# Row statistics joined on GpSimd for eight tiles at once, and value weights of two sequences from one product, spread by DMA transfers, in a decoder layer on one core

## What is computed

```python
proj = einsum('btd,ed->bte', x, W_in); gate, val = proj[..., :D], proj[..., D:]
v = depthwise_conv5(val) + conv_b
y = scan(h = tanh(a) * h + sigmoid(gate) * v)              # over the 1024 tokens
res = x + y @ W_out.T
x1 = layernorm(x + layernorm(res) * ln_w + ln_b)           # first and second norm

k, v = rmsnorm(ctx) @ Wk.T, rmsnorm(ctx) @ Wv.T            # 64 context rows a sequence
for _ in range(3):                                         # slots = x1 at first
    q = rmsnorm(slots) @ Wq.T
    attn = softmax(q @ k.T / 16, over the 1024 slots); attn /= attn.sum(over the context)
    slots = gru(attn @ v, slots)                           # gates need (attn @ v) @ gru_wih.T
x2 = layernorm(x1 + slots)
out = layernorm(x2 + x2 + x2 @ expert_w[argmax(x2 @ gate_w.T)])
```

## Time and profile before

| | |
|---|---|
| three runs | 555.04, 557.29, 557.83 us (median 557.29) |
| the profiled execution | 557.2 us, its span 555.4 us |
| mean granted TensorE clock | 0.972 |
| busy: PE, DVE, ACT, POOL | 507.8, 438.9, 343.8, 250.5 us |
| busy in the first 240 us: PE, DVE, ACT, POOL | 211.0, 200.5, 155.6, 70.6 us |

### The profile page before, as it was taken

How to read it: one execution, slowest core, us unless ns; L and a number is a source line. 1 busy time by engine, 2 the same in 40 slices (tenths; PEclk the granted TensorE clock), 3 DMA queues, 4 the chain that set the end, 5 groups by cost and what they waited for, 6 DMA issues and landing times.

```text
span 555.4 us, 7269 instructions
## 1 busy us (share of the span) xinstructions
PE 507.8 (91%) x2174; PEld 366.0 (66%) x2174; DVE 438.9 (79%) x794; ACT 343.8 (62%) x608; POOL 250.5 (45%) x217
## 2 busy tenths in 40 slices
PE   6999986978779999899999999999997999979992
PEld 2465552845557687488768867885885788767771
DVE  2899999997799477989967985897677567868783
ACT  3657539786598474667466656765663766557453
POOL 0133050400223256556935664574335156737776
PEclk9999999899898999999999999999997999989997
DMA  8960202210021032000000000002111136255752
GB/s 299 316 194 2 76 1 76 76 44 33 0 77 63 15 77 77 0 2 0 2 1 1 0 0 1 2 1 76 40 38 39 38 128 235 91 159 157 222 153 71
DMA packets 28101, 39.98 MB, mean 72 GB/s; under 512 B 7421, under 2 KB 19838, under 8 KB 27776
## 3 DMA queue, kind: packets, MB, share of 16 engines
q1 hardware_dynamic: 24656, 31.10, 18.0%
q0 software_dynamic: 3408, 8.43, 4.1%
HBM read 25.70 MB, written 16.83 MB: 77 GB/s over the span
## 4 chain that ended last, share of the span: by engine, by line
PE 51%; DVE 6%; issue 6%; POOL 4%; ACT 3%; DMA 1%; SPq 0%; POOLq 0%; ACTq 0%; DVEq 0%
PE psum L1452 35%; PE psum L1542 7%; PE psum L1255 3%; PE psum L1394 2%; PE psum L1513 2%; PE psum L1340 1%; POOL gru L1005 1%; DVE gru L1865 1%; POOL sorted_rows L1035 1%; DVE slots_full L1867 1%; POOL out L1043 1%; POOL slots_lo L1020 1%; PE psum L1352 1%; DVE gru L1845 1%; PE psum L1416 1%
## 5 line engine op out<-in xcount | busy, mean ns | idle before, releaser
L1452 PE MATMUL psum<-slots_hi,w_hh 128*128 128x512 f32 x560 | 181.5, 406 | 1.2 <-ACT gru L752 1.2
L1452 PEld LDWEIGHTS psum<-slots_hi,w_hh 128*128 128x128 f32 x560 | 104.5, 191 | 27.8 <-issue 4.2
L1005 POOL TENSOR_TENSOR gru<-slots_full,gru 128x512 f32<-128x512 f32 x43 | 65.7, 1529 | 111.8 <-ACT gru L758 111.8
L1452 PE MATMUL psum<-slots_lo,w_hh 128*128 128x512 f32 x280 | 112.0, 400 | 0.0
L1452 PE MATMUL psum<-at,v_ih_pair 128*128 128x512 f32 x288 | 91.4, 402 | 5.0 <-DVE at L1744 3.1
L758 ACT ACTIVATE gru<-gru,vec 128x512 f32<-128x512 f32 x48 | 34.7, 722 | 58.7 <-DVE gru L1845 58.6
L1452 PEld LDWEIGHTS psum<-at,v_ih_pair 128*128 128x128 f32 x288 | 53.7, 190 | 21.9 <-DVE at L1744 3.4
L1838 DVE SCALAR_TENSOR_TENSOR gru<-psum,vec,gru 128x512 f32<-128x512 f32 x48 | 35.9, 747 | 36.0 <-PE psum L1452 30.2
L1138 PE MATMUL psum<-early_hi,w_in 128*128 128x512 f32 x128 | 57.9, 611 | 5.3 <-DMA early_hi<-in_xT 5.2
L1452 PEld LDWEIGHTS psum<-slots_lo,w_hh 128*128 128x128 f32 x280 | 53.4, 191 | 12.9
L1865 DVE TENSOR_TENSOR gru<-gru 128x512 f32<-128x512 f32 x47 | 43.7, 929 | 7.2 <-POOL gru L1005 3.7
(11 more groups left out here) (249 smaller groups left out, 878.3 us busy)
## 6 DMA issues: line engine op xcount, KB each, us to landing
gathered<-sorted_rows SPq DMA_DIRECT2D x39, 129.0 KB, 2.5
x_scratch<-slots_full SPq DMA_DIRECT2D x8, 512.0 KB, 3.0
x_block<-x_scratch SPq DMA_DIRECT2D x8, 512.0 KB, 4.1
early_hi<-in_xT SPq DMA_DIRECT2D x3, 1024.0 KB, 5.4
x_tm<-in_x SPq DMA_DIRECT2D x4, 512.0 KB, 6.3
slots_full<-expert_plus SPq DMA_DIRECT2D x1, 2048.0 KB, 10.3
sorted_rows<-gru SPq DMA_DIRECT2D x1, 1032.0 KB, 11.7
early_hi<-in_xT SPq DMA_DIRECT2D x2, 512.0 KB, 4.6
```

Of the source, the lines that this page charges most:

```text
L1005: pool.tensor_tensor(DF(u), full[:, c, seq(k, h), blk(j)], X(u), ALU.subtract).then_inc(d_pool, 1)
L1452: last = pe.matmul(psum[:, bank, :], w, d, start=start and i == 0, stop=stop and i == len(pairs) - 1, skip_group_check=begun or late)
```

## The change

Statistics: bn_stats now writes to `st6` with room for both norms, and the joins leave VectorE. GpSimd makes them for eight tiles at once in six instructions (`gather_halves`): the sum of the two halves' means and spreads, the difference of the means, scaled, squared and added, and minus half the sum of the means. It also makes the offsets and mean squares (`first_offsets`, `second_offsets`). `window` and `row_roots` scale by 1/256 in their Ln. `add_bias` is split so that the first join stands ahead of its fourth addition.

Value weights: `v_sb` holds each sequence once, so one product's 128 rows are 64 of one sequence and 64 of the next; i = 0 to 3 is all there is. ScalarE copies rounded part and rest into three buffers `value_part`, used in turn (parts n = 0 to 7), and SyncE spreads each part with four transfers into `v_ih_pair`: each sequence's 64 rows to both halves of the partitions. A copy of part n > 2 waits until the four transfers of part n - 3 have landed (`vp_out`).

```diff
+        value_parts = [sb2(f"value_part{i}", [P, G3 // 2], F32R) for i in range(3)]
+        def high_part(i):
+            return 4 * (i // 2) + i % 2
+                def spread_value(pair):
+                    for n in range(4 * pair, 4 * pair + 4):
+                        w, h = n // 2 % 2, n % 2
+                        sp.wait_ge((vp_hi, vp_lo)[w], 2 * pair + h + 1)
+                        for b in range(2):
+                            for to in range(2):
+                                sp.dma_start(v_ih[pair][half(to), b, w, h * HG:(h + 1) * HG].bitcast(F32),
+                                             value_parts[n % 3][half(b), :].bitcast(F32)).then_inc(vp_out[n % 3], 16)
...
                 load_fm(3)
                 load_tm(2)
+                spread_value(0)
                 load_tm(3)
+                spread_value(1)
...
-                        act.wait_ge(agg1, NT * n1)
+                        act.wait_ge(agg1, 6 * n1)
...
+                def free_part(n):
+                    if n > 2:
+                        act.wait_ge(vp_out[n % 3], 64 * (n // 3))
...
                 def value_low(i):
-                    b, h = i // 2, i % 2
                     act.wait_ge(vp_sub, i + 1)
-                    act.activation(vp(1, b)[:, h * HG:(h + 1) * HG], psum[:, value_bank(i), 0:HG],
+                    free_part(high_part(i) + 2)
+                    act.activation(value_parts[(high_part(i) + 2) % 3][:], psum[:, value_bank(i), 0:HG],
...
-                value_high(4)
-                value_high(5)
                 first_rows(2)
-                value_low(4)
-                value_low(5)
                 new_slots(1)
                 spread_roots(0, OB)
                 low_slots(1)
-                value_high(6)
-                value_high(7)
                 window(4)
-                value_low(6)
-                value_low(7)
...
+                def gather_halves(n, done, b):
+                    even, odd = st6[:, n, :, 1:3], st6[:, n, :, 4:6]
+                    pool.tensor_tensor(joint[:, n], even, odd, ALU.add).then_inc(done, 1)
+                    pool.tensor_tensor(apart[:, n], even[:, :, 0], odd[:, :, 0], ALU.subtract).then_inc(done, 1)
+                    pool.wait_ge(done, 6 * b + 2)
+                    pool.tensor_scalar(apart[:, n], apart[:, n], 0.5 * D ** 0.5, None, ALU.mult).then_inc(done, 1)
+                    pool.wait_ge(done, 6 * b + 3)
+                    pool.tensor_tensor(apart[:, n], apart[:, n], apart[:, n], ALU.mult).then_inc(done, 1)
+                    pool.wait_ge(done, 6 * b + 4)
+                    pool.tensor_tensor(spread2[:, n], joint[:, n, :, 1], apart[:, n], ALU.add).then_inc(done, 1)
+                    pool.tensor_scalar(joint[:, n, :, 0], joint[:, n, :, 0], -0.5, None, ALU.mult).then_inc(done, 1)
...
-                add_bias(0)
+                add_bias(0, 0, H2 - 1)
+                first_spread(0)
+                first_offsets(0)
+                add_bias(0, H2 - 1, H2)
+                second_spread(0)
                 gate_product(2)
...
                 difference(0, 0)
+                second_spread(3)
+                second_offsets(3)
                 difference(0, 1)
...
-                    if q == H2 - 1:
-                        dve.wait_ge(bn1, NT * (b + 1))
-                        for t in range(NT):
-                            dve.bn_aggr(mvs[:, 0, t, :], st6[:, t, :]).then_inc(agg1, 1)
```

More of the change, by code:

```diff
@@ L158, in decoder_layer @@
         vp_mm, vp_hi, vp_sub, vp_lo = sem("vp_mm"), sem("vp_hi"), sem("vp_sub"), sem("vp_lo")
+        vp_out = [sem(f"vp_out_{i}") for i in range(3)]
         wh_hi, wh_lo = sem("wh_hi"), sem("wh_lo")
@@ L955, in _, with add_bias @@
             def _(pool):
-                def add_bias(b):
-                    for q in range(H2):
+                def add_bias(b, lo=0, hi=H2):
+                    for q in range(lo, hi):
                         j, a = 2 * q // TJ, 2 * q % TJ
@@ L989, in _ @@
                 scale_context()
-                add_bias(0)
-                gate_product(2)
-                add_bias(1)
-                gate_product(3)
-                add_bias(2)
-                add_bias(3)
+                add_bias(0, 0, H2 - 1)
[3 more added lines that the diff above has]
+                second_spread(0)
+                gate_product(2)
+                add_bias(1, 0, H2 - 1)
+                first_spread(1)
+                first_offsets(1)
+                second_offsets(0)
+                add_bias(1, H2 - 1, H2)
+                second_spread(1)
+                second_offsets(1)
+                gate_product(3)
+                add_bias(2, 0, H2 - 1)
+                first_spread(2)
+                first_offsets(2)
+                add_bias(2, H2 - 1, H2)
+                second_spread(2)
+                second_offsets(2)
+                add_bias(3, 0, H2 - 1)
+                first_spread(3)
+                first_offsets(3)
+                add_bias(3, H2 - 1, H2)
                 def difference(k, q):
@@ L1213, in value_input @@
                 def value_input(i):
-                    b, h = i // 2, i % 2
+                    pair, h = i // 2, i % 2
                     if i == 0:
@@ L1473, in unit @@
                         pe.wait_ge(at_lo, 2 * k + h + 1)
+                    if q == 0 and k < 2:
+                        for i, done in enumerate(vp_out):
+                            pe.wait_ge(done, 64 * len(range(i, 4 * k + 4, 3)))
                     run(r_bank(u), update(0), start=False).then_inc(r_mm, 1)
@@ L1762, in _ @@
                 tap_step(1, 1, 0)
-                offsets(0)
                 for i in range(1, TAPS):
@@ L1771, in _ @@
                 tap_step(2, 1, 0)
-                offsets(1)
                 for i in range(1, TAPS):
@@ L1778, in _ @@
                 taps(3, 0)
-                offsets(2)
                 residual(2)
                 tap_step(3, 1, 0)
-                offsets(3)
                 for i in range(1, TAPS):
@@ L1786, in _ @@
                 scan(3, 0)
-                offsets(4)
                 first_tops()
@@ L1792, in _ @@
                 first_product()
-                offsets(5)
                 first_attention(0)
@@ L2124, in _ @@
                 second(3, 1, 2)
-                offsets(6)
                 candidate(0, 1)
```

86 lines of the change are left out of this document (38 added, 48 removed).

## The result

| | before | after |
| --- | --- | --- |
| median, us | 556.69 (555.04 to 557.83, 4 runs) | 586.9 (583.24 to 588.14, 4 runs) |
| profiled execution, its span, us | 557.2, 555.4 | 586.3, 584.5 |
| mean granted clock of TensorE | 0.972 | 0.942 |

The ratio is 1.053 (1.048 to 1.059): 30 us slower, where 18.8 were forecast. The direction and both mechanisms were right, and the time lies above the range given.

What follows compares the result with a forecast made beforehand. Bounds: VectorE's first stage, ScalarE from 79 to 97 us, then TensorE's fixed block. 15.1 + 1.9 + 2.9 + 1.3 = +21.2, or +16.4 with shorter chains; middle +18.8 on 557.2 gives 576 us, forecast 572 to 583, wider range 562 to 583.

Steps and rivals of the forecast that it cites:

- sequence 2, statistics to rows: From the end of sequence 2's statistics to its rows: +2.7 us for the held join, less 0.8 for removed copies, +1.9.
- from there to the rows of sequence 3: Sequence 3's first norm: three VectorE attention instructions hold three join steps, so its rows start +2.9 us later.
- second norm of sequence 3: Join 1.4 us, since VectorE reading PSUM holds nothing, then roots and products: 4.9 us against 3.6, +1.3.
- taking the middle: Between +21.2 us and +16.4, where GpSimd's first two join instructions slip in ahead of the first tap: +18.8.
- the slot wait: ScalarE's fourth value copy of the second pair waits 8.9 us for part 4's transfers; 8.2 reach VectorE's third residual.
- the hold: Each of four dependent GpSimd join steps waits for the whole VectorE tap or scan under way; unheld, six instructions take 1.6 us.
- Sequence 0's term: Sequence 0's held join delays VectorE's resumption by +3.3 us, less 0.6 for the next join gone: net +2.7.
- The gain of 0.8 us: Second four value products at 112 to 130 us: ScalarE, the one waited for, loses their copies, 0.8 us of gain.
- port free: Rival: the port holds little, joins run in 1.6 us, the slot wait still costs 8.2: +6.0, 563 us; chance 0.14.
- the other side: Rival: neither port nor slot wait bites and VectorE's relief lasts to the end: -2.9, 554.3 us; chance 0.04.
- The rival without the slot wait: Only the port holds the joins: +13, or +8 with shorter chains, 565 to 570 us; within the 0.24 for between.
- Rigid block: From the scores at 229.59 us on, TensorE's almost gapless block keeps its length; the change can only move its start.

Runs made afterwards that it cites:

- stand_aside: early_parts with VectorE waiting at five places until GpSimd's join is done, no instruction added or removed: 560.0 us, ratio 1.004 to the kernel before.
- half_taps: early_parts with each VectorE tap beside a first join cut into two instructions of 512 columns (12 taps): 568.0 us, ratio 1.018 to the kernel before.
- keys_first: The changed kernel with ScalarE's key and value copies ahead of sequence 0's inverse root: 583.2 us, ratio 1.046 to the kernel before.
- early_parts: The changed kernel with the transfers of pair 1's first two value parts issued ahead of sequence 3's loads: 572.8 us, ratio 1.027 to the kernel before.
- value_early: The change's value work alone, joins on VectorE as before, pair 1's first two value parts transferred ahead of sequence 3's loads: 556.5 us, ratio 0.998.
- warm: early_parts with 20 unused matmuls of 128 by 384 in TensorE's hole ahead of sequence 1's low parts: 571.8 us, ratio 1.026 to the kernel before.
- join_only: The changed kernel's joins on GpSimd, with the value work left as in the kernel before: 572.5 us, ratio 1.026 to the kernel before.
- both_fixes: The changed kernel with the edits of early_parts and keys_first together: 570.9 us, ratio 1.024 to the kernel before.
- join_on_vector: join_only with the same six join instructions and the offsets on VectorE: 562.0 us, ratio 1.007 to the kernel before.

## Why the prediction was wrong in size

The prediction's steps, against what the two traces show (statistics of sequence 1 ended at 76.5 us before and 81.5 after, of sequence 2 at 111.45 and 130.2):

| step | forecast | measured |
| --- | --- | --- |
| join of sequence 0, rows start | 52.4 | 51.8 |
| weight product of sequence 0 | 54.4 | 53.9 |
| sequence 0 at the end of sequence 1's statistics | +2.7 | +5.0 |
| sequence 1's join to its rows | +4.2 | +3.6 |
| slot wait, at the end of sequence 2's statistics | +8.2 | +10.1 |
| sequence 2, statistics to rows | +1.9 | +2.4 |
| from there to the rows of sequence 3 | +2.9 | +5.1 |
| second norm of sequence 3 | +1.3 | +3.0 |
| sum | +21.2, lowered to +18.8 | +29.3 |

The time came out too high for the range by the sum of five misses: taking the middle (2.4 us), sequence 0's path (2.3), a clock term that the sum lacked (most of 2.2), the slot wait (1.9) and the second norm of sequence 3 (1.7). Both mechanisms, the hold and the slot wait, were right.

- **Whether the joins are held**: right, and in the long form. Taking the middle between long and short form was a loss of 2.4 us; the first instruction does not slip in ahead of the tap (44.85, 1.21 us). The runs stand_aside and half_taps show the mechanism itself.
- **Sequence 0's term** was mis-sized by 2.3 us. The step that failed is "four rows later (0.5 us each) VectorE goes on at 54.4 instead of 51.16: +3.3": the time itself was nearly right (53.92), but it followed the delay along VectorE alone. ScalarE's key and value copies stand behind the roots, so TensorE's folded product waited 4.50 us and its projection came at 55.02 instead of 48.78. keys_first, which takes that path away, has F1 3.4 us earlier: the path was the binding one.
- **The slot wait**: mechanism, part and buffer right, wait 11.15 instead of 8.9 us (9.97 where it stands alone). Two numbers were low. A transfer between SBUF tiles costs SyncE 0.64 us of issue, not the loads' 0.46; and TensorE's projection, which releases it, took 8.77 us instead of 7.28 at a granted clock that had already dropped (0.79 from 92 to 100 us). The landing was right: part 4's last issue ends at about 106.1, the copy starts at 109.31, 3.2 us, between the 2.5 and 4.1 of the earlier trace rows. The prediction's remark on the figure of the Trainium skill has its difference wrong, and the section that it names is on transfers that GpSimd issues, while these are SyncE's: 2.0 us and the bytes are 2.2 us, so the landing would be at 97.4, 0.9 us before the 98.3 that the sum uses and not 0.3. early_parts shows the whole price of the wait in this kernel, 14.1 us.
- **The gain of 0.8 us** from four copies that are gone did not show at F2 of the changed kernel. In value_early F2 is 1.0 us earlier than before although F1 is 1.0 us later, so the gain exists where nothing else is in the way.
- **A term was missing**: the removed products had kept TensorE busy while it waited for ScalarE's slots, and the held join makes that wait longer. Behind its hole of 8.69 us the granted clock is 0.56, the scores take 2.5 us more and the stage from F2 to S2 1.8 us more. This 1.8 is most of the 2.2 us by which the step to the rows of sequence 3 was too low. warm shows that the clock comes back with work in the hole; join_only, which keeps the products, loses 1.7 us in the same stage, so the removed products alone do not account for it. The prediction named the falling clock for the slot wait, but gave it no price.
- **The second norm of sequence 3**: the sentence that VectorE reading PSUM holds nothing was half right. The first five instructions took 1.3 us; the sixth and the small products behind it were held again, so the join took 2.0 us instead of the 1.4 forecast and the products 2.1 instead of 1.1:

```profile
188.04 0.75 POOL L998 TENSOR_SCALAR joint<-joint 128x8 f32<-128x8 f32 x1
189.45 0.76 POOL L1014 TENSOR_TENSOR nms<-joint,rss 128x8 f32<-128x8 f32 x1 [0.66 <-ACT rss L583]
190.16 0.20 POOL L1015 TENSOR_TENSOR rrs<-spread,rss 128x8 f32<-128x8 f32 x1
190.44 1.06 POOL L1017 TENSOR_TENSOR rrs<-rrs,rss 128x8 f32<-128x8 f32 x1
```

- **The rivals**: port free (563) and the other side (554.3) are out. The rival without the slot wait, 565 to 570, came close to what join_only measured (572.5). That VectorE waits behind GpSimd's small instructions was not seen in the taps: beside the held ones four taps took 5.46 us, against 5.42 where nothing stood beside them before.
- **Rigid block**: right. S3 is 29.3 us late, the scores of the next pair 29.6 (259.15 against 229.59), the span 29.1.

What stays open: why the granted clock fell in both_fixes beside sequence 1 and in join_on_vector ahead of the scores, and whether stand_aside with the key copies first and with work in TensorE's hole would reach the kernel before; that was not run.

## What to carry to other kernels

Price a chain of small dependent instructions on GpSimd by the length of VectorE's instructions beside it, not by its own; if it must be there, let VectorE wait for it where VectorE will wait anyway. A removed instruction may have been the work that kept TensorE's clock up (the scores took 5.8 us without it and 3.7 with other work in its place), and a buffer's release belongs in the DMA queue ahead of any load that waits for later work. Follow a delay along every engine that reads a late result, also through the instructions that merely stand behind it in a queue.

## What the runs showed of the hardware that was not expected

- The exclusion is symmetric for tiny instructions: VectorE's 0.17 us two-input instruction took 1.30 and 2.34 us behind GpSimd's work (join_on_vector; the 2.34 us stands in the kernel before too, at 103.15), while 64 single-input aggregates never took over 0.184 us.
- A single-input GpSimd instruction (TENSOR_SCALAR, 0.23 us) was held as long as a two-input one: 1.15 to 1.20 us beside taps, 2.20 beside a scan. The eight of one line in the changed kernel (duration ns min/median/max):

```profile
L993 POOL TENSOR_SCALAR apart<-apart x8: 232/1150/2197, 46.3 to 187.3; 128x8 f32<-128x8 f32 x8
```

- Adding five waits made a kernel faster by 12.8 us. A dozen useless matmuls brought sixteen others from 5.8 to 3.7 us; the 1.5 us that the time fell by is not clear of the measurement.
- Issuing a transfer of 96 KB between SBUF tiles took SyncE 0.64 us, a 512 KB load 0.46 us.
